# LayerNorm statistics in a graph kernel: aggregations put behind the next batch, and one more pair of eight pooled by GpSimd

## The reference

```python
h = maximum(layernorm(x, axis=-1), 0)            # per row of 1024: mean and variance
x_avg = transpose(h, (2, 0, 1)).mean(axis=1)     # 1024 x 128: mean over the 64 batches
x_norm = x_avg / norm(x_avg)
sim = (x_norm @ x_norm.T + 1) * 0.5              # 1024 x 1024
adj_n = (sim + gumbel0 > 1 - sim + gumbel1)
nmask = clip(adj_n + adj_n.T + eye, 0, 1)
common = nmask @ nmask.T
W = adj_n * struct(common);  Wn = dinv * W * dinv
out = x + transpose(Wn.T @ (h^T @ adj)) + bias   # for each of the 64 batches
```

## Time and profile before

| | |
|---|---|
| median of 3 runs | 809.79 us (809.56 to 809.88) |
| the profiled execution, its time | 809.41 us |
| its span | 807.6 us |
| TensorE, share of the span busy | 98% |
| VectorE, ScalarE, GpSimd | 68%, 62%, 38% |
| HBM read, written | 78.18 MB, 33.55 MB |
| granted TensorE clock over the span | 1.00 |

### The profile page before, as it was taken

The page is one execution under the profiler, slowest core; times in us unless marked ns, Lnnn a source line. Parts: engine busy times, 40 slices in busy tenths (PEclk is TensorE's granted clock), DMA queues, the critical chain, the costliest instruction groups (busy, mean ns, idle before and its releaser), DMA issues.

```text
span 807.6 us, 14263 instructions
## 1 busy us (share of the span) xinstructions
PE 793.3 (98%) x5054; PEld 449.7 (56%) x5054; DVE 551.1 (68%) x664; ACT 498.9 (62%) x529; POOL 310.9 (38%) x397
## 2 busy tenths in 40 slices
PE   8999999999999999999999999999999999999998
PEld 7887766744455555554555455545554555555553
DVE  7999877999866656665666566656665666566653
ACT  4999966786665566555655566556555666465641
POOL 5667484203333333333333333333333333333320
PEclk9999999999999999999999999999999999999999
DMA  8999941006733333333323232223222322232112
GB/s 345 408 410 409 419 178 51 2 1 245 264 116 105 106 105 104 104 104 104 104 104 100 92 114 93 98 98 111 98 94 89 121 91 93 94 115 87 53 49 83
DMA packets 29982, 112.15 MB, mean 139 GB/s; under 512 B 3456, under 2 KB 3584, under 8 KB 28928
## 3 DMA queue, kind: packets, MB, share of 16 engines
q1 hardware_dynamic: 29952, 111.75, 38.1%
HBM read 78.18 MB, written 33.55 MB: 138 GB/s over the span
## 4 chain that ended last, share of the span: by engine, by line
PE 83%; ACT 3%; DVE 2%; issue 1%; POOL 1%; POOLq 0%; ACTq 0%; DVEq 0%
PE ps L1043 68%; PE ps L959 8%; PE ps L977 2%; PE ps L1059 2%; DVE xring L1227 1%; ACT zbuf L517 1%; PE ps L828 0%; ACT a L729 0%; ACT a L717 0%; PE ps L850 0%; PE ps L995 0%; ACT xring L713 0%; PE ps L912 0%; DVE a L1345 0%; POOL zbuf L476 0%
## 5 line engine op out<-in xcount | busy, mean ns | idle before, releaser
L1043 PE MATMUL ps<-a,ybuf 128*128 128x512 f16 x2604 | 570.9, 379 | 1.1 <-DVE ybuf L1264 0.9
L1043 PEld LDWEIGHTS ps<-a,ybuf 128*128 128x128 f16 x2604 | 252.5, 98 | 297.2 <-DVE ybuf L1264 1.4
L1264 DVE TENSOR_TENSOR ybuf<-zbuf,ybuf 128x1024 f16<-128x1024 f32 x122 | 163.5, 1342 | 151.8 <-ACT ybuf L607 151.8
L471 POOL TENSOR_TENSOR zbuf<-zbuf 128x512 f32<-128x512 f32 x31 | 40.3, 1300 | 417.5 <-ACT zbuf L588 377.4
L607 ACT ACTIVATE ybuf<-zbuf 128x1024 f16<-128x1024 f32 x124 | 117.6, 950 | 110.8 <-POOL zbuf L476 96.8
L626 ACT ACTIVATE obuf<-ps,bias_sb,w_out 128x512 f32<-128x512 f32 x61 | 47.1, 772 | 110.9 <-PE ps L1043 110.9
L1253 DVE TENSOR_TENSOR hring<-hring 128x1024 f16<-128x1024 f32 x51 | 64.5, 1265 | 54.7 <-ACT hring L564 54.7
L959 PEld LDWEIGHTS ps<-w,hring 128*128 128x128 f16 x1224 | 72.5, 98 | 12.0 <-issue 0.4
L1419 DVE TENSOR_TENSOR obuf<-obuf,xring 128x1024 f32<-128x1024 f32 x63 | 77.1, 1224 | 2.7
L959 PE MATMUL ps<-w,hring 128*128 128x128 f16 x1224 | 76.7, 219 | 0.0
L588 ACT ACTIVATE zbuf<-ps 128x1024 f32<-128x1024 f32 x55 | 56.4, 1025 | 22.9 <-PE ps L959 19.7
(11 more groups left out here) (171 smaller groups left out, 688.2 us busy)
## 6 DMA issues: line engine op xcount, KB each, us to landing
xring<-in_x_dram SPq DMA_DIRECT2D x96, 512.0 KB, 4.8
out_dram<-obuf SPq DMA_DIRECT2D x63, 512.0 KB, 2.9
ybuf<-in_x_dram SPq DMA_DIRECT2D x28, 512.0 KB, 11.3
a<-in_L_gnn_gumbel_dram SPq DMA_DIRECT2D x7, 1024.0 KB, 18.5
obuf<-in_x_dram SPq DMA_DIRECT2D x9, 512.0 KB, 6.1
obuf<-in_L_gnn_gumbel_dram SPq DMA_DIRECT2D x1, 1024.0 KB, 25.9
out_dram<-obuf SPq DMA_DIRECT2D x2, 256.0 KB, 2.1
w<-in_adj_dram SPq DMA_DIRECT2D x1, 64.0 KB, 1.9
```

The source lines that it names most:

```text
L1043: mm = nc.tensor.matmul(bank[q % 2], y16[:, q % 2, yk, u, c * P:(c + 1) * P], a16[:, ak, mat, c, :], start=(start and c == yk == ak == 0), ...
L1264: nc.vector.tensor_tensor(y16[:, q % 2, 1, a:a + n, :], z[:, a + 1:a + 1 + n, :], y16[:, q % 2, 0, a:a + n, :], ALU.subtract).then_inc(s_y, 1)
```

## The change

Two things are done together.

1. `POOLED` becomes `(1, 3, 5, 7)`. In trips 0 to 2 GpSimd combines the statistics of four pairs of eight, not three; group 6 turns plain, groups 5 and 7 turn pooled. Trip 3 keeps group 1 alone. The fourth buffer for raw statistics lies at column 256 of `p5`.
2. The two `bn_aggr` of a plain pair no longer stand right behind the pair's `bn_stats`, but behind the first batch of the next pair (`moments_of` called inside the loop over j). Exceptions that keep the old order are group 0 of trip 0 and the last pairs of the trip that have no such successor. A plain pair first waits until the aggregation before the last one is done, so that its buffer is free; the last two batches wait for the aggregation of the pair before.

```diff
-POOLED = (1, 3, 6)
+POOLED = (1, 3, 5, 7)
...
-        parts = [p5[:, 24 * k:24 * k + 24].rearrange("p (b k) -> p b k", b=2) for k in range(len(POOLED))]
+        parts = [p5[:, a:a + 24].rearrange("p (b k) -> p b k", b=2) for a in (0, 24, 48, 256)]
...
+            def waits_a_batch(i, q):
+
+                last_pair = BODY1 // 2 - (2 if isinstance(i, int) and i == TRIPS1 - 1 else 1)
+                return q < last_pair and not (isinstance(i, int) and i == 0 and q == 0)
+
+            def moments_of(i, q):
+
+                dve.wait_ge(s_norm, NG * i + q + 1)
+                dve.wait_ge(s_bn, 2 * (MOMENTS * i + moments_before(q + 1, i)))
+                dve.sem_inc(s_bnseen, 1)
+                for j in (2 * q, 2 * q + 1):
+                    nc.vector.bn_aggr(moments[:, j, :], plain(i, q)[:, j % 2, :]).then_inc(s_mom, 1)
+
             def stats_of(i, q):
 
                 by_pool = pooled(i, q)
                 if by_pool:
                     dve.wait_ge(s_norm, NG * i + q + 1)
+                elif not isinstance(i, int) or MOMENTS * i + moments_before(q, i) > 2:
+                    dve.wait_ge(s_mom, MOMENTS * i + moments_before(q, i) - 2)
                 for j in (2 * q, 2 * q + 1):
+                    if j == 2 * q + 1 and q > 0 and not pooled(i, q - 1) and waits_a_batch(i, q - 1):
+                        moments_of(i, q - 1)
                     dve.wait_ge(s_x1[j], 16 * (i + 1))
                     to = parts[POOLED.index(q)][:, j % 2, :] if by_pool else plain(i, q)[:, j % 2, :]
                     for m in range(2):
                         nc.vector.bn_stats(to[:, 6 * m:6 * m + 6],
                                            x1[j][:, m * H:(m + 1) * H]).then_inc(s_bn4 if by_pool else s_bn, 1)
-                if not by_pool:
-                    dve.wait_ge(s_norm, NG * i + q + 1)
-                    dve.wait_ge(s_bn, 2 * (MOMENTS * i + moments_before(q + 1, i)))
-                    dve.sem_inc(s_bnseen, 1)
-                    for j in (2 * q, 2 * q + 1):
-                        nc.vector.bn_aggr(moments[:, j, :], plain(i, q)[:, j % 2, :]).then_inc(s_mom, 1)
+                if not by_pool and not waits_a_batch(i, q):
+                    moments_of(i, q)
...
             for j in (BODY1 - 2, BODY1 - 1):
+                dve.wait_ge(s_mom, MOMENTS * (TRIPS1 - 1) + moments_before(BODY1 // 2 - 2, TRIPS1 - 1))
                 dve.wait_ge(s_x1[j], 16 * TRIPS1)
```

## The result

The changed kernel takes 812.0 us (median of 12 runs, 811.6 to 812.19) against 809.69 us for the kernel before in the same comparison (12 runs). The ratio is 1.0027, 95% interval 1.002 to 1.0035: 2.3 us slower, where 2.2 us were forecast.

A forecast was written before the change was run, and what follows sets the result against it. GpSimd's group-to-group time becomes the first pass's bound: +0.33 (entry of trip 1), +2.29 (looped trips), +0.35 (loop edges), -0.8 (wait that goes) give +2.2 us, from 809.79 to 812.0 us; range 810.4 to 813.4 us.

The forecast's parts named there:

- Entry of trip 1: GpSimd's group 0 of trip 1 starts at about 31.35 us against 31.02 before, adding 0.33 us.
- The two looped trips with their edges: GpSimd's trips 1 and 2 take 22.64 us each, not 21.67 and 21.32: +2.29 us, plus 0.35 for two loop edges.
- The wait that goes: GpSimd's 0.90 us wait for VectorE before group 1 of trip 3 disappears, less 0.1 us of hand-over: -0.8 us.
- A looped trip of GpSimd becomes 4 x 3.91 + 4 x 1.75 = 22.64 us.: Four pooled and four plain groups make GpSimd's looped trip longer than the 20 to 21 us of the other stages.
- Loop edges 0.25 and 0.1 us: GpSimd's loop back edge after trip 1 adds 0.25 us and leaving the loop after trip 2 adds 0.1 us.
- the 1.2 us a trip that the prediction counted: GpSimd's room before the change: 20.48 us of group work in a looped trip of 21.68 us.
- Group 0 of trip 1 at 31.35, of trip 2 at 54.25, of trip 3 at 77.0; group 1 of trip 3 done at 82.1.: GpSimd's forecast times in us; before they were 31.02, 52.69 and 74.01 for the starts, 79.87 for the end.
- ScalarE stands still before batches 10 and 2: Expected sign in the profile: ScalarE stalls about 1.1 us before each of these batches, and a moment before batch 14.
- The delay goes through to the end, one for one: The first pass's later end moves everything behind it equally; last ReLU to last comparison, 96.81 to 114.43 us, stays unchanged.
- VectorE saves 3.6 us, and it buys nothing: By group 1 of trip 3: 11 moved pairs at 0.21 us plus 3 x 0.42; VectorE only runs ahead of GpSimd.
- data bind: Rival: VectorE, running earlier, may wait for transfers, which changes no time by itself; otherwise counted with the 0.12 slower case.
- ScalarE binds: Rival, chance 0.08: pooled group cost p at 3.4 us removes ScalarE's stalls, 3.3 us to be had, giving 806.5 us.

The follow-up runs named there:

- the two halves: Kernel before with only the aggregations moved, POOLED (1, 3, 6): 808.5 us; kernel before with only the fourth pooled pair, aggregations in place: 812.15 us.
- the two shorter chains: Whole change with GpSimd's pooled chain reordered to wait less, same instruction count: 807.7 us; whole change with three instructions taken out of that chain: 806.28 us.
- the interleaved chain: GpSimd's pooled variance in as many instructions, ordered so most wait for the last but one; on the whole change 807.7 us, ratio 0.9975 against the kernel before.

## Why the prediction was right

The forecast was that GpSimd's time from group to group becomes the bound, and that is what happened. Its size is in part luck. Between the traces the end of group 1 of trip 3 moved by 82.50 - 79.87 = 2.63 us, where 2.2 were forecast. Entry of trip 1: +0.47 us (forecast 0.33). The two looped trips with their edges: 23.18 - 21.67 and 22.78 - 21.32, together +2.97 us (forecast 2.29 + 0.35). The wait that goes: -0.81 us (forecast -0.8). Only the 0.3 us by which the traced execution before was fast bring the medians to 2.3 us. Step by step:

- *A looped trip of GpSimd becomes 4 x 3.91 + 4 x 1.75 = 22.64 us.* Measured 23.18 and 22.78 us from group 0 to group 0, edges in. A pooled group took 3.91 to 3.92 us, once 4.02 us (44.61 to 48.63 us).
- *Loop edges 0.25 and 0.1 us.* The back edge was mis-sized: 54.67 - 54.15 = 0.52 us, where 0.16 us are usual, so 0.36 us. This and the one slow group make trip 1 0.3 us longer than forecast. The exit costs 0.07 us. The prediction took both to lie under waits for VectorE before. But the same idle stretches, 0.53 and 0.23 us, stand before and after the earlier trace rows; so before, too, the edges were GpSimd's own time, or very nearly so. They come off its room: of the 1.2 us a trip that the prediction counted, 0.7 us were waits for VectorE. These are the two of trip 1 before (0.17 us of each are usual):

```profile
33.44 0.21 POOL L405 TENSOR_TENSOR p<-p 128x4 f32<-128x4 f32 x1 [0.83 <-DVE p L1143]
...
46.58 0.20 POOL L405 TENSOR_TENSOR p<-p 128x4 f32<-128x4 f32 x1 [0.22 <-DVE p L1143]
```

That fits the lengthening: 2.16 us more load less 0.7 us is 1.46 us, and the trips grew by 1.51 and 1.46 us.

- *Group 0 of trip 1 at 31.35, of trip 2 at 54.25, of trip 3 at 77.0; group 1 of trip 3 done at 82.1.* Measured 31.49, 54.67, 77.45 and 82.50. The 0.4 us are the back edge and the slow group (0.2 us together) and 0.14 us at the start of trip 1. That this start came so close is luck: group 2 of trip 0 began at 15.95 us and not at 15.7, the groups behind it took 0.2 us less than the sum had, and the entry of the loop cost 0.18 us and not 0.05 to 0.1.
- *ScalarE stands still before batches 10 and 2.* Seen, with 1.14 and 1.04 us, and 0.81, 1.42 and 0.46 us. The moment before batch 14 is there too, inside a merged row: the three ReLUs of batches 12 to 14 take 3.73 us in both looped trips, where they took 3.49 us before.
- *The delay goes through to the end, one for one.* 17.63 against 17.62 us from the last ReLU to the last comparison, and 2.6 us on the span.
- *VectorE saves 3.6 us, and it buys nothing.* That it buys nothing is shown by the two halves: +2.3 us with or without the moved aggregations. The size was too high. At the end of pair 1 of trip 3 VectorE stood at 72.22 + 1.24 = 73.46 us, and in the trace before at 76.16 us; that is 2.7 us. The term per pair was about right (0.18 us left of 0.42, where 0.21 was forecast); pair 0 of trip 3 is moved as well, so that by its own terms the sum was 3.8 us. What was missing is the pace of the transfers, which the prediction had named as the case "data bind", and which, as said there, changed no time by itself. So VectorE ended its statistics at 88.01 + 1.26 = 89.27 us and not at about 88.
- *The rival "ScalarE binds" needs p = 3.4 us or less.* That is what the two shorter chains did: at 3.40 us 2.0 us faster, at 3.07 us 3.5 us faster. The rival's 3.3 us were well sized; its point of decision lies a little under 3.4 us, as the sum for it left the loop's edge out.

So both edits do what they say, and the sum is a loss because one of them loads an engine that had 0.7 us to spare in a trip with 2.2 us. The moved aggregations alone are 1.3 us faster than before, and GpSimd takes the rest of their worth. The best versions with the full computation that were run are the interleaved chain with three pooled groups, (1, 3, 6) or (0, 3, 6), 2.7 us faster.

What stays open: with the interleaved chain, whether two or three pooled groups are better, and which of the sets is best, is within the intervals. Why one pooled group of trip 1 takes 0.1 us more than the others, before and after, was not looked into.

## What to carry to other kernels

On an engine that runs short instructions which wait for one another, measure from the start of one unit of work to the start of the next while its input lies ready; busy time left out a quarter of GpSimd's load here, and the 38% over the whole span said nothing of the first pass. Before moving work from one stage of a balanced pipeline to another, add up the receiving stage for a whole trip with the new mix, loop edges included, and compare it with the slowest stage, not with its own idle time. A stage that gets faster can leave the next one as the bound: here GpSimd capped the worth of the moved aggregations even without a fourth pooled pair. Interleaving independent steps of such a chain gave back 0.5 us of 3.9 with the same number of instructions.

## What the runs showed of the hardware beyond what was expected

- Between small GpSimd instructions (2 to 8 columns), the start-to-start time is 0.15 us without a wait for the result just before and 0.28 us with one (39.94 to 40.09 and 40.23 to 40.51 us with the interleaved chain); a busy time of 0.20 us is shown for each in both cases.
- GpSimd's loop back edge costs 0.36 us (0.52 us idle, where 0.16 us are usual), and its exit less than 0.1 us. The idle stretch at the back edge is 0.53 us in the kernel before, in the one after, and in those with the aggregations moved or the fourth pair alone, whether or not the bracket names VectorE.
- Two `bn_aggr` right behind the `bn_stats` that they read cost 0.42 us, and 0.18 us with one more batch's `bn_stats` in between.
